# Perceiver layer on one core: the router reads raw rows and takes its normalisation afterwards, units from step 127 on, one pass for the last eight groups

## The reference

```python
def _layernorm(x, axis=-1, eps=1e-05):
    m = jnp.mean(x, axis=axis, keepdims=True)
    v = jnp.var(x, axis=axis, keepdims=True)
    return (x - m) / jnp.sqrt(v + eps)
...
    xf = x.reshape(-1, D)
    logits = xf @ Wr.T + br
    expert_idx = jnp.argmax(logits, axis=-1)
    h = jax.nn.relu(jnp.einsum('td,efd->etf', xf, W1) + b1[:, None, :])
    y = jnp.einsum('etf,edf->etd', h, W2) + b2[:, None, :]
    out = y[expert_idx, jnp.arange(xf.shape[0])]
...
x = x + _L0_xattn_ref(_layernorm(x, axis=-1), ctx_768, ...)
x = x + _L0_attn_ref(_layernorm(x, axis=-1), ...)
x = x + _L0_ffn_ref(_layernorm(x, axis=-1), ...)
```

## Time and profile before

| | us |
|---|---|
| median of 3 runs | 953.63 (951.38 to 954.02) |
| profiled execution | 950.45 |
| its span | 948.7 |
| PE / DVE / ACT / POOL busy in the span | 858.7 / 806.1 / 683.1 / 788.3 |
| mean granted clock of TensorE, share of 2.4 GHz | 0.954 |

### The profile page before, as it was taken

How to read it: one execution, slowest core, us unless ns; L and a number is a source line. 1 busy time by engine, 2 the same in 40 slices (tenths; PEclk the granted TensorE clock), 3 DMA queues, 4 the chain that set the end, 5 groups by cost and what they waited for, 6 DMA issues and landing times.

```text
span 948.7 us, 28634 instructions
## 1 busy us (share of the span) xinstructions
PE 858.7 (91%) x8486; PEld 712.5 (75%) x8486; DVE 806.1 (85%) x2058; ACT 683.1 (72%) x1956; POOL 788.3 (83%) x1218
## 2 busy tenths in 40 slices
PE   7999999999999999999999999999999874429992
PEld 7777787887888888888888888888887663427882
DVE  5899879898989898989898989989898967657882
ACT  3877787777878787887877787877887662308881
POOL 5798898989898989998999989898989754654885
PEclk9999999999999999999999999999999985659997
DMA  9122222222211221222221222112120032111220
GB/s 251 26 60 73 61 61 61 61 61 61 60 59 59 59 59 59 75 62 75 64 78 59 59 59 59 59 59 59 59 60 28 1 122 105 43 51 49 73 64 13
DMA packets 56704, 60.90 MB, mean 64 GB/s; under 512 B 8750, under 2 KB 50609, under 8 KB 56640
## 3 DMA queue, kind: packets, MB, share of 16 engines
q1 hardware_dynamic: 54144, 55.84, 20.2%
q0 software_dynamic: 2496, 4.26, 1.4%
HBM read 37.65 MB, written 23.34 MB: 64 GB/s over the span
## 4 chain that ended last, share of the span: by engine, by line
PE 35%; POOL 32%; issue 14%; DVE 11%; ACT 4%; POOLq 1%; SPq 1%; DMA 0%; DVEq 0%; ACTq 0%
POOL Pn L1040 12%; PE bank L392 7%; PE bank L443 5%; PE bank L414 4%; PE bank L436 4%; POOL cT L1031 3%; PE bank L404 3%; PE bank L420 3%; POOL out_dram L1430 3%; POOL chi L1021 2%; POOL e12p L1047 2%; DVE Tl L885 2%; POOL clo L1025 2%; POOL e12p L1050 1%; POOL yb L1424 1%
## 5 line engine op out<-in xcount | busy, mean ns | idle before, releaser
L813 ACT ACTIVATE Pe<-bank,nmax 128x257 f32<-128x257 f32 x512 | 241.5, 472 | 108.2 <-DVE nmax L881 89.2
L1040 POOL TENSOR_TENSOR Pn<-Pe,rsum 128x1028 f32<-128x1028 f32 x128 | 243.1, 1900 | 36.3 <-DVE rsum L905 28.8
L392 PE MATMUL bank<-cT,qh 96*128 96x257 f16 x1024 | 184.3, 274 | 5.7 <-ACT Pe L813 4.1
L885 DVE TENSOR_TENSOR Tl<-bank,Th 128x1024 f16<-128x1024 f32 x128 | 155.4, 1214 | 2.3 <-ACT Th L802 1.9
L443 PE MATMUL bank<-identf,Pn 128*128 128x128 f32 x1024 | 152.7, 275 | 0.6 <-POOL Pn L1040 0.4
L802 ACT ACTIVATE Th<-bank 128x512 f16<-128x512 f32 x256 | 141.0, 593 | 9.1 <-PE bank L443 9.0
L392 PE MATMUL bank<-cT,ql 96*128 96x257 f16 x512 | 139.1, 272 | 0.0
L392 PEld LDWEIGHTS bank<-cT,qh 96*128 96x128 f16 x1024 | 97.6, 97 | 44.9 <-issue 9.6
L443 PEld LDWEIGHTS bank<-identf,Pn 128*128 128x128 f32 x1024 | 114.2, 141 | 9.1 <-POOL Pn L1040 2.1
L881 DVE TENSOR_REDUCE nmax<-bank 128x2 f32<-128x514 f32 x128 | 88.1, 688 | 21.0 <-PE bank L392 19.9
L894 DVE TENSOR_REDUCE nmax<-bank 128x1 f32<-128x257 f32 x256 | 105.0, 412 | 0.0
(11 more groups left out here) (229 smaller groups left out, 2431.3 us busy)
## 6 DMA issues: line engine op xcount, KB each, us to landing
sorted_rows<-fill SPq DMA_DIRECT2D x30, 589.5 KB, 3.8
rawT<-in_dram SPq DMA_DIRECT2D x32, 385.5 KB, 4.5
raw<-in_dram SPq DMA_DIRECT2D x32, 384.0 KB, 5.1
xs<-sorted_rows SPq DMA_DIRECT2D x23, 131.0 KB, 2.2
R<-in_dram SPq DMA_DIRECT2D x4, 512.0 KB, 5.8
Z<-last_rows SPq DMA_DIRECT2D x128, 2.2 KB
w1r<-in_dram SPq DMA_DIRECT2D x4, 512.0 KB, 8.0
w2fr<-in_dram SPq DMA_DIRECT2D x4, 512.0 KB, 9.2
```

What stands on the lines that cost most here:

```text
L392: last = nc.tensor.matmul(bank[SB[t]][:, 0:M], w[:, par, b, t * P:(t + 1) * P], cT[:, s4, c, 0:M], start=(k == 0), stop=(k == 2))
L813: nc.scalar.activation(Pe[:, n_par(j + 1), t, :], bank[SB[t]][:, 0:M], ACT.Exp, bias=nmax[:, n_par(j + 1), t:t + 1], accum_out=sums[:, n_p ...
L885: nc.vector.tensor_tensor(Tl[:, n_par(j - 1), :, :], psum[:, 4:4 + MC, :], Th[:, n_par(j - 1), :, :], ALU.subtract).then_inc(s_Tl, 1)
L1040: nc.gpsimd.tensor_tensor(Pn[:, par, :, :], Pe[:, par, :, :], rsum[:, par, :].unsqueeze(2).broadcast_to([P, QT, M]), ALU.mult)\
```

## The change

The rows are no longer normalised before the router. With m the mean of a row, r its reciprocal standard deviation, W the router's weights and b its bias, the kernel now computes r (x W) + (-m r) (sum of W) + b. In detail:

- `act_unit_norm`, `dve_norm` and their 32 instructions are gone; `pe_unit_T` transposes raw rows of `X`, which only needs the chunks of the time mixing (`m_res`), not the statistics.
- The sum of W comes from one product with a matrix of ones (line 493 of the new kernel), which DVE copies to `wsum` in step 127.
- Unit 0 is transposed in step 127; in each of steps 128 to 132 PE transposes the next unit and multiplies the one before; behind step 133 come the product of unit 5, and transposes and product of unit 6. Transposes write banks 0 and 1, products banks 2, 4, 5 and 6.
- ACT copies `x3T` in steps 128 to 132 and after, its weight halves (16 instructions) stand together behind step 140.
- DVE multiplies each unit's products by r (line 714) and adds the offsets of a whole half with three wide operations (`dve_offsets`, `dve_add_offsets`). Units 0 to 2 are done in step 131, 3 to 5 behind step 134.
- The rank products of the first half stand behind the transposes of chunk 15 on PE; on DVE `dx`, `mdx`, `xm` of chunk 15 stand directly behind the first half's ranks.
- Statistics of groups 24 to 31 are made in one pass at the end, in place of two passes of four groups. All 16 of DVE's weight halves come after `pk`.
- `pe_warm(6, 7)` is gone, the last `pe_warm(14)` is `pe_warm(20)`.

```diff
-            if n_static(n) == B + 3:
+            if n_static(n) == B - 1:
+                wait(nc.tensor, s_rw, 32)
+                wait(nc.tensor, s_raw0, 3)
+                wait(nc.tensor, s_exp, QT * B)
+                nc.tensor.matmul(bank[2][:, 0:E], onesf[:, :], wrT[:, :], start=True, stop=True).then_inc(s_ws, 1)
                 pe_unit_T(0)
-            if n_static(n) == B + 4:
-                pe_unit_T(1)
-                pe_unit_logits(0)
+            if n_static(n) is not None and B <= n < B + UA - 1:
+                wait(nc.tensor, s_ws, 2)
+                pe_unit_T(n - B + 1)
+                pe_unit_logits(n - B)
...
+            nc.gpsimd.memset(onesf[:, :], 1.0).then_inc(s_raw0, 1)
...
-        LB = (0, 1, 2, 6)
-
-        def x3_bank(i):
-            return 4 + i % 2
+        LB = (2, 4, 5, 6)
+        UT = 2
 
         def pe_unit_T(i):
 
+            wait(nc.tensor, s_exp, QT * B)
+            wait(nc.tensor, s_m["res"], UT * (i + 1))
+            wait(nc.tensor, s_f["xc"], i - 1)
+            for t in range(CT):
+                last = nc.tensor.transpose(bank[i % 2][:, t * P:(t + 1) * P], X[:, CT * i + t, :], identf[:, :])
+            last.then_inc(s_f["xT"], 1)
...
-            wait(nc.tensor, s_f["xc"], i - 1)
-            wait(nc.tensor, s_f["xn"], i + 1)
-            pe_norm_T(i % 2, x3_bank(i), s_f["xT"])
-
-        def pe_unit_logits(i):
-
-            b = LB[i % 4]
-            wait(nc.tensor, s_exp, QT * B)
-            wait(nc.tensor, s_Ol, B)
+            if i >= 3:
+                wait(nc.tensor, s_Ol, B)
             wait(nc.tensor, s_f["lg"], i - 3)
             wait(nc.tensor, s_f["xc"], i + 1)
             wait(nc.tensor, s_rw, 32)
             for t in range(CT):
-                last = nc.tensor.matmul(bank[b][:, P + t * E:P + (t + 1) * E], x3T[:, i % 2, t * P:(t + 1) * P],
+                last = nc.tensor.matmul(bank[LB[i % 4]][:, P + t * E:P + (t + 1) * E], x3T[:, i % 2, t * P:(t + 1) * P],
                                         wrT[:, :], start=True, stop=True)
             last.then_inc(s_f["rt"], 1)
...
-        def act_unit_norm(i):
-
-            wait(nc.scalar, s_f["xT"], i - 1)
-            wait(nc.scalar, s_nmr, 1 + max(0, i - UA + 1))
-            for t in range(CT):
-                k = CT * i + t
-                last = nc.scalar.activation(xn[:, i % 2, t, :], X[:, k, :], ACT.Identity, bias=nmr[:, k:k + 1],
-                                            scale=rst[:, k:k + 1])
-            last.then_inc(s_f["xn"], 1)
-
         def act_unit_x3T(i):
 
             wait(nc.scalar, s_f["rt"], i - 1)
             wait(nc.scalar, s_f["xT"], i + 1)
-            nc.scalar.activation(x3T[:, i % 2, :], bank[x3_bank(i)][:, :], ACT.Copy).then_inc(s_f["xc"], 1)
+            nc.scalar.activation(x3T[:, i % 2, :], bank[i % 2][:, :], ACT.Copy).then_inc(s_f["xc"], 1)
...
-            b = LB[i % 4]
-            wait(nc.vector, s_rw, 32)
+            wait(nc.vector, s_lnc, ln3.count)
             wait(nc.vector, s_f["rt"], i + 1)
-            nc.vector.tensor_tensor(lg[:, CT * i:CT * (i + 1), :],
-                                    bank[b][:, P:P + CT * E].rearrange("p (t e) -> p t e", e=E),
-                                    brb[:, :].unsqueeze(1).broadcast_to([P, CT, E]), ALU.add)\
-                .then_inc(s_f["lg"], 1)
+            sl = slice(CT * i, CT * (i + 1))
+            nc.vector.tensor_tensor(lg[:, sl, :], bank[LB[i % 4]][:, P:P + CT * E].rearrange("p (t e) -> p t e", e=E),
+                                    rst[:, sl].unsqueeze(2).broadcast_to([P, CT, E]), ALU.mult).then_inc(s_f["lg"], 1)
+
+        def dve_offsets(a, b, half):
+
+            wait(nc.vector, s_nmr, half + 1)
+            wait(nc.vector, s_ws, 2)
+            wide = [P, b - a, E]
+            nc.vector.tensor_tensor(lgc[:, a:b, :], nmr[:, a:b].unsqueeze(2).broadcast_to(wide),
+                                    wsum[:, :].unsqueeze(1).broadcast_to(wide), ALU.mult).then_inc(s_lgc, 1)
+            wait(nc.vector, s_lgc, 3 * half + 1)
+            nc.vector.tensor_tensor(lgc[:, a:b, :], lgc[:, a:b, :], brb[:, :].unsqueeze(1).broadcast_to(wide), ALU.add)\
+                .then_inc(s_lgc, 1)
+
+        def dve_add_offsets(a, b, half):
+
+            wait(nc.vector, s_lgc, 3 * half + 2)
+            wait(nc.vector, s_f["lg"], -(-b // CT))
+            nc.vector.tensor_tensor(lg[:, a:b, :], lg[:, a:b, :], lgc[:, a:b, :], ALU.add).then_inc(s_lgc, 1)
+            wait(nc.vector, s_lgc, 3 * half + 3)
 
...
-            if n_static(n) in (B + 2, B + 3, B + 4):
-                i = n_static(n) - B - 2
-                act_unit_norm(i)
-                if i:
-                    act_unit_x3T(i - 1)
+            if n_static(n) is not None and B <= n < B + UA - 1:
+                act_unit_x3T(n - B)
...
+            if n_static(n) == B - 1:
+                wait(nc.vector, s_ws, 1)
+                nc.vector.tensor_copy(wsum[:, :], bank[2][:, 0:E]).then_inc(s_ws, 1)
             if n_static(n) == B + 1:
                 dve_rstd(0, GA, 0)
+            if n_static(n) == B + 3:
+                dve_unit_logits(0)
+                dve_unit_logits(1)
+                dve_unit_logits(2)
...
-        def dve_norm(i):
-
-            wait(nc.vector, s_f["xT"], i - 1)
-            for t in range(CT):
-                k = CT * i + t
-                last = nc.vector.tensor_scalar(xn[:, i % 2, t, :], X[:, k, :], mean[:, k:k + 1], rst[:, k:k + 1],
-                                               ALU.subtract, ALU.mult)
-            last.then_inc(s_f["xn"], 1)
...
-                pool.wait_ge(s_row, 3 if half == 0 else 7)
+                pool.wait_ge(s_row, 3 + 2 * half)
...
+            act_unit_x3T(UA - 1)
+            act_unit_x3T(UA)
             drain(act_step, LIT, 5, 7)
-            for i in range(3, UA):
-                act_unit_norm(i)
-                act_unit_x3T(i - 1)
-            act_unit_x3T(UA - 1)
             drain(act_step, LIT + 1, -1, 5)
-            act_std(GA, GA + CT, 1)
-            act_unit_norm(UA)
 
             def act_w(ks):
                 for k in ks:
@@ -1461,13 +1469,11 @@
                     act.wait_ge(s_w3r[k // 4], 32)
                     nc.scalar.activation(dst[:, k // 2, :], src[:, k // 2, :], ACT.Copy).then_inc(s_w3h, 1)
 
-            act_w(range(0, 8))
+            act_w(range(2 * E))
             drain(act_step, LIT + 1, 5, 7)
-            act_unit_x3T(UA)
-            act_w(range(8, 2 * E))
             drain(act_step, LIT + 2, -1, 7)
-            act_std(GA + CT, G, 2)
             act_unit_x3T(UA + 1)
+            act_std(GA, G, 1)
...
-            for i in range(2, UA):
-                pe_unit_T(i)
-                pe_unit_logits(i - 1)
             pe_unit_logits(UA - 1)
-            pe_rank(0, GA, 0)
-            drain(pe_step, LIT, 6, 7)
-            drain(pe_step, LIT + 1, -1, 6)
             pe_unit_T(UA)
             pe_unit_logits(UA)
-            drain(pe_step, LIT + 1, 6, 7)
+            drain(pe_step, LIT, 6, 7)
+            drain(pe_step, LIT + 1, -1, 1)
+            pe_rank(0, GA, 0)
+            drain(pe_step, LIT + 1, 1, 7)
             drain(pe_step, LIT + 2, -1, 5)
             pe_warm(8, 7)
             drain(pe_step, LIT + 2, 5, 6)
-            pe_warm(6, 7)
...
-            pe_warm(14)
+            pe_warm(20)
...
-            for i in range(UA):
+            dve_offsets(0, GA, 0)
+            for i in range(3, UA):
                 dve_unit_logits(i)
-            dve.wait_ge(s_f["lg"], UA)
+            dve_add_offsets(0, GA, 0)
             dve_hot(0, GA)
             dve.wait_ge(s_ftab, 12)
             dve_rank(0, GA, 0)
-            drain(dve_step, LIT + 1, -1, 1)
             mix_dx(nc.vector, LIT + 1, 0)
             mix_xm(nc.vector, LIT + 1, 1)
-            drain(dve_step, LIT + 1, 1, 2)
+            drain(dve_step, LIT + 1, -1, 2)
             mix_out(nc.vector, LIT + 1, 1)
-            for j in range(2, 4):
+            for j in range(2, 6):
                 dve_step(LIT + 1, j)
                 mix_states(nc.vector, LIT + 1, j)
-            dve_var(GA, GA + CT, 1)
-            drain(dve_step, LIT + 1, 4, 5)
-            mix_states(nc.vector, LIT + 1, 4)
-            dve_rstd(GA, GA + CT, 1)
-            drain(dve_step, LIT + 1, 5, 6)
-            mix_states(nc.vector, LIT + 1, 5)
-            dve_w(range(0, 4))
             drain(dve_step, LIT + 1, 6, 7)
             drain(dve_step, LIT + 2, -1, 2)
             mix_out(nc.vector, LIT + 2, 1)
+            drain(dve_step, LIT + 2, 2, 7)
+
+
+            dve_var(GA, G, 1)
+            dve_rstd(GA, G, 1)
+            dve_offsets(GA, G, 1)
             dve_unit_logits(UA)
-            drain(dve_step, LIT + 2, 2, 7)
-
-
-            dve_var(GA + CT, G, 2)
-            dve_rstd(GA + CT, G, 2)
-            wait(dve, s_nmr, 3)
-            wait(dve, s_lnc, ln3.count)
-            dve_norm(UA + 1)
             dve_unit_logits(UA + 1)
-            dve.wait_ge(s_f["lg"], CH)
```

(3 more changed lines are left out.)

6 lines of the change are left out of this document (added).

## The result

The kernel with the change takes **940.0 us** (median of 4 runs, 939.3 to 940.6), the kernel before 952.5 (4 runs, 949.0 to 954.0). The ratio is 0.9875, with a 95% interval of 0.9855 to 0.9895: 10 to 14 us faster, 12.5 by the medians, against the forecast 12.9 and 940.7. The profiled execution has a span of 938.3 against 948.7, 10.4 less.

A forecast was written before the change was run, and what follows sets the result against it. The way from step 127 to the first expert tile was the bound, with SP's block-number loads deciding by 4.4 us. 14.4 - 3.2 + 1.7 = 12.9 us off 953.63 gave 940.7, range 935.0 to 946.5.

The forecast's parts named there:

- Part 1: First six router units, raw rows in steps 128 to 132: first half's places at 786.5, 5.6 us earlier.
- 3.4 us of covered idle time: PE's idle time before `pe_y` of steps 129 to 131, expected to cover as much of three blocks' 6.6 us.
- Part 2: POOL's gap between the two scatter runs shrinks from 4.8 to 0.30, second places near 814: 4.5 us gained.
- Landing: Last scatter's landing, ahead of the first fetch, forecast at 833.4 instead of 843.47.
- a term that I had put at nothing: Last eight scatters beside DVE's weight halves: 1 us lost, set off against scatters slow beside the four early halves.
- The rule of the Trainium skill: Exclusive port lock of VectorE against GpSimd: all eight last scatters held up, gain near 10 us; forecast expected perhaps five.
- Part 3: SP's block-number loads end at 832.3 and no longer decide; the fetch waits for the scatters, 14.4 us earlier.
- Part 4: Twenty unread products after the last landing take 6.7 and hold PE until 840.1: 3.2 us given back.
- The first tile at full clock: First tile follows the unread products at full clock; its transposes and products save 1.7 us.
- (a): Rival: only POOL's gap closes, first places stay at 792.1; 7.3 us left, 946.3; chance 0.16.
- (b): Rival: blocks hide wholly, clock stays full, unread products faster; 3.2 and 2 us more, 935.5; chance 0.14.
- (c): Rival: clock stays low in steps 129 to 133, places 10 us later, 956.2; chance 0.05.

The follow-up runs named there:

- e3_units_behind: Changed kernel with the router units' transposes and products back in their old places, raw rows and later order kept; 941.9 us, ratio 0.9895 to the kernel before.
- e4_halves_after_landing: Changed kernel with DVE's 16 weight halves held back until the last scatter has landed; 942.7 us, ratio 0.9906 to the kernel before.
- e8_products_between: Changed kernel with the twenty unread products moved behind DVE's last weight half, eight more in PE's first-tile waits; 937.0 us, ratio 0.9844 to the kernel before.

## Why the prediction was right

The total is right, 12.9 against 11.9 aligned and 12.5 by the medians; the pieces beneath it are less so. That the time itself, 940.7, came so close to 940.0 is in part luck: the median of before that it was taken from lies 1.1 above the one measured with the result.

- **Part 1, places 5.6 earlier.** Measured 5.0 (787.05 aligned, forecast 786.5). Chunk 13's sum was forecast at 777.9 and came at 779.39 - 1.47 = 777.9, and the clock was full in 769 to 773 as said; step 131's `pe_y` came 2.5 later (forecast 3.2). What the text left unsaid, `e3_units_behind` showed: 4.0 of the 5.0 stay without the early start, on whose 3.4 us of covered idle time the working rested. The forecast had gone by DVE's queue from chunk 13's sum on, in which both causes look alike.
- **Part 2, no gap.** Right: 0.30 before the 25th scatter, the second places at 815.1 (forecast 814). The list of reasons was too long. With the tail in its old order they still come in time, if only just.
- **Landing.** Aligned 834.3 against the forecast 833.4. 0.5 are the late places. The rest is a term that I had put at nothing: I had set off the 1 us of the last eight scatters against the early four halves. The last eight took 835.75 - 821.50 = 14.25 to the landing, against 843.47 - 830.34 = 13.13 before, 1.1 more; the first 24 took 31.6 (789.60 to 821.20) against 32.4, 0.8 less. That leaves 0.3.
- **The rule of the Trainium skill**, SBUF — State Buffer, section "SBUF: two separate sides". Six of the eight were held up, and all six that ran beside halves, by 0.17 once and 0.52 five times; the two behind the last half were not. That is nearer to the rule than "perhaps five". Whether a scatter is stopped until one half ends or only slowed, these rows don't tell: 0.52 is a little less than the 0.60 of a half, halves stood behind each other without a break for 9.7 us, and scatters went on beside them at two thirds of their pace. For a tensor operation of POOL the trace of `e4_halves_after_landing` agrees with the rule's full block: 6.35 in place of 0.70.
- **Part 3.** Right, and shown from both sides by the pair of runs with the loads apart. The fetch goes out at 835.78 - 1.47 = 834.3, 13.5 earlier than before (forecast 14.4).
- **Part 4, given back 3.2.** Measured 13.5 less the 9.9 by which the transposes are earlier: 3.6. Twenty products took 7.2 and not 6.7, since half clock held longer. The two runs that take this wait away got 2.2 to 2.6 of it back.
- **The first tile at full clock, 1.7.** From the transposes to the first `yout` it is 1.3 (11.95 against 13.27), and another 0.6 by the end, whose cause no run shows. Nor need all of the 1.3 be the clock: `e8_products_between`, also at full clock, but with its transposes starting as the rows come, took 12.47 for the same way. `e4_halves_after_landing` gives the price from the other side: a start 1.3 later than the changed kernel's, at the lower clock, ended 3.2 later.

So 13.5 - 3.6 + 1.3 + 0.6 = 11.8 stand for 14.4 - 3.2 + 1.7 = 12.9. The median of before lies above its profiled execution by 2.05, the median after at it (940.0 and 940.09); taking off the offset of 1.47 makes up for most of that, and 0.6 are left between 12.5 and 11.9. Of the rivals, (a) needed first places at 792.1, and they came at 787.05; (b) needed blocks that hide wholly, where step 131 came 2.5 later, and shorter unread products, which took 7.2; (c) needed places 7 us late.

## What to carry to other kernels

Where a small product waits for a normalisation, apply the normalisation to the product: what it frees is the engine that made the rows, and moving the product earlier as well may add little (1.0 of 5.0 here). A stretch of dummy work that holds the clock up belongs where the engine waits anyway, and its end should be set against the arrival of what it waits for. Before crediting a reordering with a gain, undo it alone, and ask what hides its worth: the order of part 2 brought the rows 3.2 forward, into a wait for unread products. And when a serial stretch is moved off the start, compare it with the lead that the buffers give where it lands.
